# Attention values as stationary operand: y comes out of TensorE transposed, with reciprocals transposed instead of y

## What is computed

```python
x = x + 0.5 * ffn(layernorm(x))     # 2 of 8 routed experts with capacity, and a shared expert
x = x + attention(layernorm(x))     # 16 heads of 16, causal within groups of 64 tokens
x = x + 0.5 * ffn(layernorm(x))

# attention, per group of 64 tokens
q, k, v = split(xg @ w_qkv)                       # q and k: rmsnorm over all 256, times ln_w
att = softmax(causal(q @ k.T / sqrt(16)))         # per head, 64 x 64
y   = att @ v                                     # 64 x 16 per head, 16 heads side by side
out = y @ w_proj
```

## Time and profile before

| | us |
|---|---|
| median of 3 runs | 2122.65 |
| lowest and highest run | 2120.07, 2126.28 |
| the profiled execution, its own time | 2113.96 |
| its span, first to last instruction | 2112.2 |

### The profile page before, as it was taken

One profiled execution on the slowest core, in us unless ns is written; L12 is line 12 of the kernel. 1 busy time (PEld: TensorE's weight loads), 2 busy tenths in 40 slices (PEclk: granted clock), 3 DMA queues, 4 the chain that ended last, 5 costly groups with the idle time before them and its releaser, 6 DMA issues.

```text
span 2112.2 us, 37639 instructions
## 1 busy us (share of the span) xinstructions
PE 2082.5 (99%) x13844; PEld 1912.4 (91%) x13844; DVE 1360.0 (64%) x3108; ACT 962.3 (46%) x1910; POOL 493.1 (23%) x433
## 2 busy tenths in 40 slices
PE   9999999999999999999999999999999999999999
PEld 7888899999998788888887888888999999988888
DVE  7666556666665688888888876665566666633333
ACT  3333335555553565655665542333455555523232
POOL 2423211121212233223334433322021211200000
PEclk9999999999999999999999999999999999999999
DMA  9331225554436344444455432221244444531010
GB/s 275 104 115 59 76 64 132 134 141 113 106 86 198 81 118 112 111 118 98 113 116 131 121 109 75 79 90 48 82 106 111 103 102 104 125 115 60 30 61 21
DMA packets 295976, 218.70 MB, mean 104 GB/s; under 512 B 69241, under 2 KB 276525, under 8 KB 295792
## 3 DMA queue, kind: packets, MB, share of 16 engines
q1 hardware_dynamic: 278128, 194.92, 32.9%
q0 software_dynamic: 17664, 21.38, 5.7%
HBM read 129.48 MB, written 93.23 MB: 105 GB/s over the span
## 4 chain that ended last, share of the span: by engine, by line
PE 89%; DVE 6%; issue 2%; ACT 1%; DMA 1%; SPq 1%; POOL 0%; DVEq 0%; ACTq 0%
PE gate_up_p L353 29%; PE quad L353 25%; PE out_p L391 22%; PE misc L391 4%; PE quad L576 2%; PE quad L561 2%; PE misc L545 1%; PE quad L577 1%; PE misc L417 1%; DVE h_s L1044 1%; PE misc L428 1%; PE misc L426 1%; PE misc L409 1%; DMA stage<-in_L_ffn_rd 1%; DVE p_s L1179 1%
## 5 line engine op out<-in xcount | busy, mean ns | idle before, releaser
L353 PE MATMUL gate_up_p<-zh,w 128*128 128x512 f32 (+2 forms) x2368 | 703.1, 359 | 2.0 <-DVE h_s L1044 1.4
L731 ACT CAST hh<-h_s 128x512 fp32r<-128x512 f32 (+2 forms) x511 | 276.2, 541 | 671.1 <-DVE h_s L1044 654.3
L353 PE MATMUL quad<-zh,w 128*128 128x512 f32 (+2 forms) x1728 | 481.7, 346 | 0.0
L353 PEld LDWEIGHTS gate_up_p<-zh,w 128*128 128x128 f32 x2368 | 429.9, 189 | 49.8 <-DVE h_s L1044 2.4
L391 PE MATMUL out_p<-w,hh 128*128 128x256 f32 x2808 | 458.8, 282 | 6.6 <-DVE hl L1128 5.2
L391 PEld LDWEIGHTS out_p<-w,hh 128*128 128x128 f32 x2808 | 403.8, 189 | 28.9 <-DVE hl L1128 9.0
L353 PE MATMUL gate_up_p<-zl,w 128*128 128x512 f32 (+2 forms) x1184 | 421.4, 356 | 0.0
L1044 DVE TENSOR_TENSOR h_s<-gate_up_p,sg_s 128x512 f32<-128x512 f32 (+2 forms) x296 | 178.4, 603 | 246.6 <-PE gate_up_p L353 244.6
L1060 DVE TENSOR_TENSOR hl<-h_s,hh 128x512 fp32r<-128x512 f32 (+2 forms) x431 | 247.1, 573 | 136.4 <-ACT hh L731 120.9
L353 PEld LDWEIGHTS quad<-zh,w 128*128 128x128 f32 x1728 | 308.5, 188 | 24.6
L353 PE MATMUL quad<-zl,w 128*128 128x512 f32 (+2 forms) x864 | 295.4, 342 | 0.0
(11 more groups left out here) (189 smaller groups left out, 2532.8 us busy)
## 6 DMA issues: line engine op xcount, KB each, us to landing
stage<-in_L_ffn_rg SPq DMA_DIRECT2D x128, 128.0 KB, 2.8
stage<-in_L_ffn_ru SPq DMA_DIRECT2D x128, 128.0 KB, 3.0
stage<-in_L_ffn_rd SPq DMA_DIRECT2D x128, 128.0 KB, 3.2
heads_d<-qkh SPq DMA_DIRECT2D x128, 128.0 KB
q_t<-heads_d SPq DMA_DIRECT2D x32, 384.0 KB, 4.6
k_t<-heads_d SPq DMA_DIRECT2D x64, 192.0 KB, 4.8
slots_d<-empty SPq DMA_DIRECT2D x16, 662.5 KB, 7.4
zh_d<-zh SPq DMA_DIRECT2D x16, 512.0 KB, 3.2
```

The lines of the kernel that those rows point to most:

```text
L353: last = pe.matmul(dst, a, b, start=(k == 0), stop=(k == 3 * n - 1))
L731: nc.scalar.copy(hh[:, n % 2, 0:ncol], h_s[:, n % 2, 0:ncol]).then_inc(sm["hh_done"], 1)
```

## The change

- `values`: the values are the stationary operand, 66 columns at a time (`vv` gets four columns of padding at its end), the probabilities move: per pair of heads `vh` with `ph`, `vh` with `pl`, `vl` with `ph`, 128 columns each, added in PSUM. y comes out with heads and their numbers on partitions and tokens along the row: 24 matmuls for 16.
- `y_transpose` is gone. `inverse_sums` writes every reciprocal 16 times (`rden` is 128 x 16 x 16), `inverse_transposes` turns this on TensorE behind `scores`, and ScalarE copies it to `rdt`, behind the second silu of the step.
- `outputs`: eight products of 32 partitions x 2 x 64, PSUM times `rdt`, in place of two reductions and a product. They pick the blocks that belong to their own tokens.
- `yh` is copied from `y_s` in SBUF; `yl` is a subtraction on GpSimd, first in its step.
- `quarter_s` is gone: the quarter sums go into the front of `half_s`.
- Order: row sums and reciprocals stand behind `qke` in every step, also with c = 0; the drained steps (no more qkv) have an order of their own on VectorE; GpSimd's `piece_low` of a step stands before the subtraction of the maximum and waits for `qkl`; the first steps of the pipeline are ordered a little otherwise.

The core of the diff:

```diff
-        vv = sb("vv", [P, VDEEP, NH // 2, 2, 64], F32R, att)
+        vv = sb("vv", [P, VDEEP, NH * 64 + 4], F32R, att)
...
-        rden = sb("rden", [P, NH], F32, att)
-        y_s = sb("y_s", [P, C], F32, att)
+        rden = sb("rden", [P, NH, HD], F32, att)
+        rdt = sb("rdt", [P, KC, P], F32, att)
+        y_s = sb("y_s", [P, KC, P], F32, att)
...
+        def vv_at(rows, q, part):
+            return vv[rows, q, 0:NH * 64].rearrange("p (j a c) -> p j a c", a=2, c=64)[:, :, part, :]
...
-            def y_transpose(t):
-                pe.wait_ge(sm["a_yn"], t + 1)
+            def inverse_transposes(t):
+                pe.wait_ge(sm["a_rden"], t + 1)
+                pe.wait_ge(sm["a_pl"], t + 1)
                 for k in range(KC):
-                    last = pe.transpose(quad[:, 1, k * P:(k + 1) * P], y_s[:, k * P:(k + 1) * P], ident[:, :])
-                last.then_inc(sm["a_yt"], 1)
+                    o = C + k * P
+                    last = pe.transpose(misc[:, 1, o:o + P], rden[:, NH // KC * k:NH // KC * (k + 1), :].rearrange("p h d -> p (h d)"), ident[:, :])
+                last.then_inc(sm["a_rt"], 1)
...
-                    pe.matmul(quad[:, j // 4, o:o + P], ph[:, j, :], vv[:, q, j, :, :].rearrange("p a c -> p (a c)"), start=True, stop=False)
-                    last = pe.matmul(quad[:, j // 4, o:o + 64], pl[:, j, :], vv[:, q, j, 0, :], start=False, stop=True)
+                    dst = quad[0:GROUP + 2, j // 4, o:o + P]
+                    vh, vl = (vv[:, q, (2 * j + a) * 64:(2 * j + a) * 64 + GROUP + 2] for a in range(2))
+                    pe.matmul(dst, vh, ph[:, j, :], start=True, stop=False)
+                    pe.matmul(dst, vh, pl[:, j, :], start=False, stop=False)
+                    last = pe.matmul(dst, vl, ph[:, j, :], start=False, stop=True)
...
-                if out is not None:
-                    y_transpose(out)
...
-                if probs is not None and keys is not None:
+                if out is not None and keys is not None:
                     prob_transposes(probs, z, uses)
...
                 if keys is not None and probs is not None:
                     scores(keys, z, out)
+                if probs is not None:
+                    inverse_transposes(probs)
                 up(n + 1, b % 2, c + 1, buf, SB)
...
-                    act.wait_ge(sm["a_yt"], out + 1)
+                    act.wait_ge(sm["a_yn"], out + 1)
                     wait(act, sm["a_x"], out)
-                    nc.scalar.copy(yh[:, :, :], chunks(quad[:, 1, 0:C])).then_inc(sm["a_yh"], 1)
+                    nc.scalar.copy(yh[:, :, :], y_s[:, :, :]).then_inc(sm["a_yh"], 1)
...
+                if probs is not None:
+                    act.wait_ge(sm["a_rt"], probs + 1)
+                    wait(act, sm["a_yn"], probs)
+                    nc.scalar.copy(rdt[:, :, :], chunks(misc[:, 1, C:2 * C])).then_inc(sm["a_rr"], 1)
...
             def outputs(t):
                 dve.wait_ge(sm["a_y"], t + 1)
-                wait(dve, sm["a_yt"], t)
-                yp = quad[:, :, :].rearrange("p b (j a c) -> p (b j) c a", a=2, c=64)
+                dve.wait_ge(sm["a_rr"], t + 1)
+                wait(dve, sm["a_yl"], t)
                 for g in range(2):
-                    rows = slice(64 * g, 64 * g + 64)
-                    last = v.tensor_reduce(y_s[rows, :].rearrange("p (j c) -> p j c", c=2 * HD), yp[rows, :, 32 * g:32 * g + 32, :], AX, ALU.add)
-                last.then_inc(sm["a_ysum"], 1)
-                dve.wait_ge(sm["a_rden"], t + 1)
-                dve.wait_ge(sm["a_ysum"], t + 1)
-                y_heads = y_s[:, :].rearrange("p (h d) -> p h d", d=HD)
-                v.tensor_tensor(y_heads, y_heads, rden[:, :].unsqueeze(2).broadcast_to([P, NH, HD]), ALU.mult).then_inc(sm["a_yn"], 1)
+                    tokens = slice(GROUP * g, GROUP * g + GROUP)
+                    for m in range(4):
+                        rows = slice(32 * m, 32 * m + 32)
+                        own = quad[32 * g:32 * g + 32, :, m * P + GROUP * g:m * P + GROUP * g + GROUP]
+                        last = v.tensor_tensor(y_s[rows, :, tokens], own, rdt[rows, :, tokens], ALU.mult)
+                last.then_inc(sm["a_yn"], 1)
...
                 dve.wait_ge(sm["a_den"], t + 1)
-                wait(dve, sm["a_yn"], t)
-                v.reciprocal(rden[:, :], den_a[:, :]).then_inc(sm["a_rden"], 1)
+                wait(dve, sm["a_rt"], t)
+                v.reciprocal(rden[:, :, :], den_a[:, :].unsqueeze(2).broadcast_to([P, NH, HD])).then_inc(sm["a_rden"], 1)
...
-                if out is not None:
-                    dve.wait_ge(sm["a_yh"], out + 1)
-                    v.tensor_tensor(yl[:, :, :], chunks(quad[:, 1, 0:C]), yh[:, :, :], ALU.subtract).then_inc(sm["a_yl"], 1)
...
                     h_product(n, SB)
+                    if probs is not None:
+                        prob_low(probs)
+                    fused_low(n)
+                    if probs is not None:
+                        row_sums(probs)
+                        inverse_sums(probs)
+                    if keys is not None:
+                        masked(keys)
...
-                if probs is not None and c:
+                if probs is not None and not drained:
                     row_sums(probs)
                     inverse_sums(probs)
-                heads_first = z is not None and (c == 0 or out is None)
+                heads_first = z is not None and c == 0
...
-                if probs is not None and not c:
-                    row_sums(probs)
-                    inverse_sums(probs)
...
+                if out is not None:
+                    pool.wait_ge(sm["a_yh"], out + 1)
+                    g.tensor_tensor(yl[:, :, :], y_s[:, :, :], yh[:, :, :], ALU.subtract).then_inc(sm["a_yl"], 1)
                 if probs is not None:
...
+                if 0 <= refill(s) < NCH:
+                    pool.wait_ge(sm["a_qkl"], z + 1)
+                    piece_low(refill(s))
                 if keys is not None:
                     pool.wait_ge(sm["a_max"], keys + 1)
                     g.tensor_tensor(p_s[:, :, :], p_s[:, :, :],
                                     smax[:, :].unsqueeze(2).broadcast_to([P, NH, GROUP]), ALU.subtract).then_inc(sm["a_sub"], 1)
-                if 0 <= refill(s) < NCH:
```

More of the change, by code:

```diff
@@ L607, in fused_step @@
                     qkv(z, out)
+                if probs is not None and out is None:
+                    prob_transposes(probs, z, uses)
                 up(n, b % 2, c, buf, SB)
@@ L616, in fused_step @@
                     scores(keys, z, out)
+                if probs is not None:
+                    inverse_transposes(probs)
                 up(n + 1, b % 2, c + 1, buf, SB)
-                if keys is not None and probs is None:
-                    scores(keys, z, out)
                 if any(block_at(pf, step, pb, c) is not None for step in ("T", "R", "M")):
-                    wait(pe, sm["a_pl"], probs + 1 if probs is not None else upto(s, -LAG["probs"]))
+                    wait(pe, sm["a_rr"], probs + 1 if probs is not None else upto(s, -LAG["probs"]))
                     wait(pe, sm["a_qkl"], upto(s, 1 - LAG["z"]))
@@ L629, in fused_step @@
                 assert all(block_at(pf, step, pb, c + 1) is None for step in ("T", "R", "M"))
+                if keys is not None and probs is None:
+                    scores(keys, z, out)
                 if ahead is not None:
@@ L778, in values_high @@
                         o = 32 * g + HD * r
-                        last = nc.scalar.copy(vv[64 * r:64 * r + 64, t % VDEEP, :, 0, o:o + HD], src)
+                        last = nc.scalar.copy(vv_at(slice(64 * r, 64 * r + 64), t % VDEEP, 0)[:, :, o:o + HD], src)
                 last.then_inc(sm["a_vh"], 1)
@@ L1270, in fused_step @@
                     normal(ahead)
-                if not heads_first:
+                if not heads_first and not drained:
                     fused_low(n)
@@ L1436, in fused_step @@
                 f, phase, b, c = fused_chunk(s)
-                z, keys, probs, ahead = (tile_at(s, stage) for stage in ("z", "keys", "probs", "stats"))
+                z, keys, probs, out, ahead = (tile_at(s, stage) for stage in ("z", "keys", "probs", "out", "stats"))
                 n = chunk(f, phase, b, c)
+                if out is not None:
+                    pool.wait_ge(sm["a_yh"], out + 1)
+                    g.tensor_tensor(yl[:, :, :], y_s[:, :, :], yh[:, :, :], ALU.subtract).then_inc(sm["a_yl"], 1)
                 if probs is not None:
```

28 lines of the change are left out of this document (14 added, 14 removed).

## The result

| | before | after |
|---|---|---|
| median of the runs (4 and 4), us | 2121.38 | 2175.32 |
| lowest and highest | 2120.07, 2126.28 | 2175.13, 2181.99 |
| the profiled execution, its span | 2113.96, 2112.2 | 2175.17, 2173.4 |

The ratio is 1.0254, with an interval of 1.0235 to 1.0274: the change makes the kernel slower by 54 us. I had forecast 24 us slower, and 2166 as the upper end of the range. The direction was right; the loss that I forecast is less than half of the measured one, and the time lies 9 us above the range.

A forecast was written before the change was run, and what follows sets the result against it. TensorE, busy 99%, was taken to bound the kernel, with VectorE under 3 us to spare per plain step. 13.7 + 8.8 + 5.1 - 3.9 = 23.7 us on 2113.96 gave 2137.7, with 8.7 to the median 2146; range 2118 to 2166.

The forecast's parts named there:

- the reciprocal decides: VectorE, fused stage: the reciprocal grows from 128x16 to 128x256 and takes 1753 ns, 1.50 us more per tile.
- Rival 1: Reciprocal streams like the sum at 0.41 us, so TensorE is the bound again: faster, 2115.7 us; chance 0.13.
- rival 2: VectorE's waits of 2.1 us in a step take up all of its 1.5: no change, 2122 us; chance 0.13.
- Rival 3: Narrow products at the 2.66 bound or a reciprocal some 0.5 us dearer: 2162 us and up; chance 0.16.
- a plain step: Fused step with c not 0: 0.65 us longer, ending at 16.95 and not 16.31; 21 x 0.65 = 13.7 us.
- one with c = 0: Fused step where sums and reciprocal now stand ahead of the first value split: 1.1 us longer; 8 x 1.1 = 8.8.
- One link: Plain step: `yl` on GpSimd was let start when VectorE's `hl` ends, at 0.96 us after `outputs`.
- there VectorE has few pauses, so they pay the full 1.5 and not 0.65: Six of the 21 steps with c not 0, those with routing work: 5.1 us more in all.
- the start order at nothing: First steps of the pipeline: the prediction's sum has no term for their changed order.
- an estimated 3.9 in four steps: GpSimd's weight piece, now ahead of the maximum, no longer blocks VectorE's product and `hl`: 3.9 us gained.
- the drained steps at nothing: Three last steps, without qkv and head transposes: TensorE and VectorE have room there, so their new order costs nothing.
- nobody waits for the transposes of the reciprocals: TensorE behind the scores: the two new transposes take 0.22 us; their inputs are done before the scores can start.

The follow-up runs named there:

- first experiment: The changed kernel with VectorE taking 16 reciprocals per row again and ScalarE writing the 16 copies; 2121.52 us, ratio 1.0021 to the kernel before.

## Why the prediction was right in direction and wrong in size

**Right: the reciprocal decides, and its price.** 1753 ns were forecast and measured, and without it the loss goes (first experiment). Rival 1 (0.41 us, faster) falls by the group's row; rival 2 (the waits take up all) by 0.87 of 1.5 on the mean of steps 9 to 25. Rival 3 would have given the time, but not by its reasons: neither the reciprocal nor the narrow products are dearer than I took them.

**Right: a plain step and one with c = 0.** 16.95 forecast, 16.87 to 17.0 measured; + 1.1 forecast, + 1.24 measured in steps 9 to 25 (18.45 against 17.21). The plain steps of before take 16.45 to 16.52 over the stretch and not the 16.31 of the step that I read, so the difference is 0.45 and not 0.65. The order of waits inside a plain step came as forecast. In after, from the end of `outputs` at 971.85, `h_s` starts at 7.18 (7.35 forecast), the causal add at 11.45 (11.6) and `outputs` at 14.54 (14.65):

```profile
979.03 0.63 DVE L1059 TENSOR_TENSOR h_s<-gate_up_p,sg_s 128x512 f32<-128x512 f32 x1
...
986.39 2.36 DVE L1211 TENSOR_TENSOR y_s<-quad,rdt 32x128 f32<-32x128 f32 x8
```

One link was wrong and cost little: `yl` follows `yh` and not `hl` (above); `hl` itself ends at 1.05 by the earlier trace rows, not at the 0.96 that I wrote. The same wait that I had named decides the step with c = 0 (after):

```profile
960.57 1.75 DVE L1226 RECIPROCAL rden<-den_a 128x256 f32<-128x256 f32 x1
962.24 0.52 DVE L1171 TENSOR_TENSOR vv<-quad,vv 64x128 fp32r<-64x128 f32 x2
963.70 0.42 PEld L540 LDWEIGHTS misc<-ident,qk 128*128 128x128 f32 x4 [1.50 <-DVE qk L1179]
```

**Wrong, the main step: "there VectorE has few pauses, so they pay the full 1.5 and not 0.65".** The ground was right and the term mis-sized: 8.6 us for steps 26 to 35 against 30.9. Two things were left out. All ten steps pay about the full 1.5 on the mean, not six of them; with the clock mostly held they lose 18.6 us (experiment with unused matmuls), of which some 4 would belong to the weight piece (188.3 against 184.0 us above, with the short reciprocal). And behind TensorE's stalls of up to 3.4 us there its clock falls from 2.4 to 1.2 GHz for a while, in spells that the filled stalls mostly take away: at least 12.3 us more. I had followed the chain from VectorE to TensorE and stopped there, with TensorE's own durations taken as given; that its matmuls would take longer after a stall was in none of my cases. The earlier trace rows had the hint: the step with routing work has 0.98 for the clock already, the plain one 1.00.

**Wrong: the start order at nothing.** Step 7 is 8.7 us longer. Before, then after:

```profile
719.70:736.30 16.60, 16.53 (x109) 14.35 (x108) 12.53 (x25) 10.02 (x21) 5.20 (x6) 0.96 0.40 96
...
719.00:744.40 25.40, 19.54 (x115) 17.03 (x116) 16.21 (x32) 10.62 (x21) 7.03 (x6) 0.80 0.29 69
```

TensorE's loads wait 3.9 us for `hl` and 3.5 for `qk` there, nothing and 0.4 before, and the clock is 0.80. It is the order and not the reciprocal: with the old order the step takes 17.7 us, and with the new order and a short reciprocal in this step it took 21.5 in one profile and 25.6 in another (long for the late tiles). Which of the moves brings the waits was not tried apart. With a short reciprocal the new start costs 2 to 4 us; with a long one what the old start gains is lost again later.

**Wrong in sign: "an estimated 3.9 in four steps" for the weight piece.** It costs about 4. I priced the block that goes, and not the subtraction of the maximum, which now stands behind 1.85 us of work; the rows of step 30 above show it.

**Wrong: the drained steps at nothing.** From step 36 to the end 9.0 us were lost, by my terms 1.1; the experiment with the long reciprocal for the late tiles puts 6.2 of them down to the reciprocal. I named the condition (room on both engines) and did not look at it, and that nobody waits for the transposes of the reciprocals does not hold there. After, from 1272.9 on:

```profile
PEld misc L513 <- DVE rden L1226: 5.8, 2, 3.7
```

**The range.** I added 0.4 us a step for my errors. What failed was not noise of the steps but three places (start, late steps, drained steps) taken for like the step that I had read, and all three failed to the same side.

## What to carry to other kernels

Price an operation whose time grows steeply with its elements by the slope of two of its sizes, and where only copies of few results are wanted, keep it narrow and let an engine with room write the copies: 1.5 us on VectorE became 0.4 us elsewhere, and nearly all of 54 us of loss went with it. Where a slower engine makes a nearly saturated TensorE wait, look at the granted clock of that stretch: a stall can be paid twice. Read a step from each part of a pipeline (start, busiest steps, drain) and not its steady part alone, since the same 1.5 us cost 1.0 in one part and 2.6 in another.

## What the runs showed of the hardware that was not expected

- TensorE idle for 15.3 of 294.0 us left the clock at 1.00, idle for 25.7 of 214.9, with single waits of the loads of up to 3.4 us, went with 0.90. 160 matmuls that nobody needs, put into those waits, brought it back to 0.98 and the ten steps from 214.9 to 202.6 us. But with `yl` on VectorE it was 0.97 at 27.0 us idle of 204.7, with a longest wait of 3.4 us: what sets it beyond that is open.
- A reciprocal on VectorE takes 178, 253 and 1753 ns for 4, 16 and 256 elements a row: a straight line, 6.25 ns an element. A copy that repeats each element 16 times takes 410 ns for 256 on ScalarE and 400 on GpSimd.
- Matmuls with 66 columns of weights and 128 moving follow each other at 0.065 us on the mean of 24, with 128 columns of weights at 0.111.
